# Moving mask products, diagonal chunks and low-part products within TensorE's order in an attention kernel

## What is computed

```python
q = (_rms_norm(x @ w_qa, q_a_norm_w) @ w_qb)          # 16 heads, 128 plain + 64 rotary features
kv = x @ w_kva                                        # 64 latent + 64 rotary features
...
scores = jnp.einsum('bhsd,bhtd->bhst', q_full, k_full) * scale
mask = jnp.tril(jnp.ones((seq, seq), bool))
scores = jnp.where(mask[None, None], scores, jnp.finfo(scores.dtype).min)
attn = jax.nn.softmax(scores, axis=-1)
out = jnp.einsum('bhst,bhtd->bhsd', attn, v)
return out.transpose(0, 2, 1, 3).reshape(b, seq, H * D_V) @ w_o
```

## Time and profile before

| | before |
|---|---|
| median of 3 executions | 1333.49 us (1332.36 to 1334.62) |
| the profiled execution, its own time | 1329.14 us |
| its span | 1327.3 us |
| mean granted clock of TensorE, as a share of 2.4 GHz | 0.958 |
| TensorE matmul busy, of the span | 1208.6 us, 91% |
| VectorE, ScalarE, GpSimd busy | 889.2, 790.8 and 688.2 us |

### The profile page before, as it was taken

One profiled execution on the slowest core, in us unless ns is written; L12 is line 12 of the kernel. 1 busy time (PEld: TensorE's weight loads), 2 busy tenths in 40 slices (PEclk: granted clock), 3 DMA queues, 4 the chain that ended last, 5 costly groups with the idle time before them and its releaser, 6 DMA issues. The chain is left out here.

```text
span 1327.3 us, 23952 instructions
## 1 busy us (share of the span) xinstructions
PE 1208.6 (91%) x9452; PEld 957.0 (72%) x9452; DVE 889.2 (67%) x1836; ACT 790.8 (60%) x1166; POOL 688.2 (52%) x569
## 2 busy tenths in 40 slices
PE   2765999999999999999999999999999867989897
PEld 2653677777777677777777777777777666878886
DVE  2533776776676777767677776767766567677676
ACT  1163467777777777777777777777787733222222
POOL 0122366667666666766666676666676742111100
PEclk9876799999999999999999999999999987999899
DMA  9202010000100200110020010002000040000000
GB/s 276 75 0 64 9 42 17 1 17 28 31 17 1 58 2 17 31 28 17 2 58 1 17 36 23 17 1 58 2 17 2 1 159 1 1 16 1 17 17 16
DMA packets 57679, 39.65 MB, mean 30 GB/s; under 512 B 7744, under 2 KB 57152, under 8 KB 57408
## 3 DMA queue, kind: packets, MB, share of 16 engines
q1 hardware_dynamic: 51216, 33.94, 8.8%
q10 hardware_dynamic: 6352, 4.19, 1.3%
HBM read 33.66 MB, written 4.46 MB: 29 GB/s over the span
## 5 line engine op out<-in xcount | busy, mean ns | idle before, releaser
L777 DVE TENSOR_REDUCE gates<-bank 128x1 f32<-128x512 f32 (+3 forms) x640 | 384.5, 608 | 218.8 <-PE bank L850 144.9
L669 POOL TENSOR_TENSOR pt_lo<-pt 128x1024 f16<-128x1024 f32 x192 | 371.1, 1938 | 227.8 <-ACT pt L726 227.0
L726 ACT ACTIVATE pt<-pair 128x1024 f32<-128x1024 f32 x192 | 196.3, 1023 | 135.8 <-PE pair L875 134.7
L717 ACT ACTIVATE pair<-shift 128x1024 f32<-128x1024 f32 x256 | 263.4, 1029 | 12.2 <-ACT pt L730 0.4
L893 PE MATMUL bank<-values,pt 128*128 128x129 f16 x2176 | 235.1, 222 | 10.1 <-DVE rowsum L809 10.0
L893 PEld LDWEIGHTS bank<-values,pt 128*128 128x128 bf16 x2176 | 191.5, 97 | 62.2 <-issue 34.4
L895 PE MATMUL bank<-values,pt_lo 128*128 128x65 f16 x2176 | 223.8, 192 | 0.0
L675 POOL TENSOR_TENSOR pt_lo<-pt 128x512 f16<-128x512 f32 (+3 forms) x256 | 178.8, 721 | 72.1 <-ACT pt L730 71.6
L895 PEld LDWEIGHTS bank<-values,pt_lo 128*128 128x128 f16 x2176 | 193.8, 98 | 0.0
L730 ACT ACTIVATE pt<-pair 128x512 f32<-128x512 f32 (+3 forms) x256 | 111.5, 437 | 76.9 <-PE pair L878 76.5
L875 PE MATMUL pair<-q_hi,kt_a_hi 128*128 128x512 f32 (+1 forms) x320 | 134.6, 421 | 0.0
(11 more groups left out here) (217 smaller groups left out, 2331.0 us busy)
## 6 DMA issues: line engine op xcount, KB each, us to landing
turn_by<-rope_cos_by_feature SPq DMA_DIRECT2D x64, 128.0 KB, 3.0
turn_by<-rope_sin_by_feature SPq DMA_DIRECT2D x64, 128.0 KB, 3.1
xs<-in_L_attn_x ACTq DMA_DIRECT2D x1, 2048.0 KB, 24.9
lat<-in_L_attn_w_o SPq DMA_DIRECT2D x1, 2048.0 KB, 26.3
xs_again<-in_L_attn_x SPq DMA_DIRECT2D x1, 2048.0 KB, 8.1
out<-xs_again SPq DMA_DIRECT2D x4, 512.0 KB, 2.8
lat<-in_L_wmod SPq DMA_DIRECT2D x1, 1536.0 KB, 15.7
lat<-in_L_attn_w_qb SPq DMA_DIRECT2D x1, 1152.0 KB, 7.6
```

The costliest lines, as they stand in the source:

```text
L669: pool.tensor_tensor(out=pt_lo[:, at].rearrange("p a n -> p (a n)"), in0=full, in1=cut(full), op=ALU.subtract).then_inc(low_ok, 1)
L717: act.activation(s_pair[u % 2][:, :, :], shift[:, item % SHIFTS:item % SHIFTS + 1, :].to_broadcast([P, 2, BW]), ACT.Copy).then_inc(seeded[ ...
L726: act.activation(pt[:, at], s_pair[u % 2][:, :, :], ACT.Exp).then_inc(exp_done, 1)
L777: dve.tensor_reduce(out=mx[:, item % MAXIMA, t, part:part + 1], in_=work_of(w)[:, 0:n * P], axis=AXX, op=ALU.max).then_inc(work_seen["v"], 1)
```

## The change

Three edits. In `scores`, both mask products of a diagonal unit are issued before the unit's first score product, behind the wait for the seed and ahead of the wait for the low part of the queries; the product with the stop flag is now the third score product. In the plan, the chunks of an item are put in another order: the rounds of the chunk numbers stay as they are, but the four diagonal chunks take those numbers that are last in a round of at least two chunks with no shift rows and no query products (`before_values`: there `weigh` follows directly); where an item has fewer than four such places, its earliest other numbers fill up. In `weigh`, the product with the low part comes before the one with the high part. No operation, wait or byte is added or taken away.

```diff
+def before_values(c):
+    r = CHUNK_ROUND[c]
+    return c == CHUNKS_AT[r][-1] and len(CHUNKS_AT[r]) > 1 and r not in SHIFT_AT and PREP_AT.get(r, (0, 3))[1] == 3
+
+for _k in range(NI):
+    _at = range(FIRST_CHUNK[_k], FIRST_CHUNK[_k + 1])
+    _rest = [CHUNKS[c] for c in _at if CHUNKS[c][2] != ITEMS[_k][1]]
+    _diagonal = [CHUNKS[c] for c in _at if CHUNKS[c][2] == ITEMS[_k][1]]
+    _places = sorted(_at, key=lambda c: not before_values(c))[:BT]
+    for _c in _at:
+        CHUNKS[_c] = (_diagonal if _c in _places else _rest).pop(0)
...
                         pe.wait_ge(seeded[e], SEEDS[e][u + 1])
+                        for n in range(0 if d is None else 2):
+                            on = (d + n) * P
+                            pe.matmul(s_pair[u % 2][:, n, on:on + P], mask16[:, :], ident16[:, :], start=False, stop=False,
+                                      skip_group_check=True)
                         if u == FIRST_UNIT[item]:
                             pe.wait_ge(q_lo_ok, item + 1)
...
-                        last = pe.matmul(to, keys[a], q[b], start=False, stop=(m == 2 and d is None), skip_group_check=True)
-                    if d is not None:
-                        on = (d + half) * P
-                        last = pe.matmul(s_pair[u % 2][:, half, on:on + P], mask16[:, :], ident16[:, :], start=False, stop=True,
-                                         skip_group_check=True)
+                        last = pe.matmul(to, keys[a], q[b], start=False, stop=(m == 2), skip_group_check=True)
                     last.then_inc(s_done, 1)
...
-                            pe.matmul(to[:, col:col + 2 * KVL + 1], cut(pt[:, at, half, mine]), values[:, j + half, 0:2 * KVL + 1],
+                            pe.matmul(to[:, col + KVL:col + 2 * KVL + 1], pt_lo[:, at, half, mine], values[:, j + half, KVL:2 * KVL + 1],
                                       start=(u == FIRST_UNIT[item] and half == 0 and t % 2 == 0), stop=False, skip_group_check=True)
-                            last = pe.matmul(to[:, col + KVL:col + 2 * KVL + 1], pt_lo[:, at, half, mine],
-                                             values[:, j + half, KVL:2 * KVL + 1], start=False, stop=end, skip_group_check=True)
+                            last = pe.matmul(to[:, col:col + 2 * KVL + 1], cut(pt[:, at, half, mine]),
+                                             values[:, j + half, 0:2 * KVL + 1], start=False, stop=end, skip_group_check=True)
```

## The result

| | before | after |
|---|---|---|
| median | 1333.86 us (4 runs, 1332.36 to 1334.62) | 1312.74 us (4 runs, 1310.41 to 1314.08) |
| ratio, 95% interval | | 0.9843 (0.9828 to 0.9859) |
| the profiled execution and its span | 1329.14 and 1327.3 us | 1310.41 and 1308.6 us |
| first to last value product (the attention stage) | 155.99 to 1067.66: 911.7 us | 157.46 to 1050.21: 892.8 us |
| all the rest of the span | 415.7 us | 415.9 us |

The change is faster by 21.1 us of the medians, 18.7 us of the two spans. The forecast was 15.3 us and 1318 us; the range 1305 to 1327 holds the result. All of the spans' difference lies in the attention stage. That stage is the finer measure here: a second profile of the changed kernel gave 892.7 us for it (another 0.1 us apart), while the rest took 420.6 us instead of 415.9.

What follows compares the result with a forecast made beforehand. TensorE's queue was taken to bound attention; masks 13.4, low part first 2.9 and chunk order -1.0 summed to 15.3 us, so 1333.49 - 15.3 = 1318 us. The range for 8 in 10 was 1305 to 1327.

Steps and rivals of the forecast that it cites:

- The bound: Attention: TensorE busy 891.7 of 910 us at full clock, so attention costs what its queue costs.
- Masks in front: Diagonal units: two masks behind the value products share one return to fp32r; 20.5 us at most, 13.4 us kept.
- The split by the wait for VectorE: Diagonal rounds: 61 gain 0.16 us each; of 67 with late work, 52 keep 0.04 and 15 keep 0.10.
- Low part first: 192 units off the diagonal: 129-column value product last before fp32r, step 0.04, 2.9 us gained, between 0 and 5.8.
- the estimate by the Trainium skill: Low part first: fp32r load hides behind the whole longer product, 27 ns x 192 = 5.2 us gained instead of 2.9.
- Diagonal chunks last: Chunk order: TensorE gains 1 us, VectorE loses 2; together 1 us lost, between 4 gained and 5 lost.
- VectorE's loss: Rounds with shifts and queries: maxima of full chunks move in, 0.3 x 7 such rounds, 2 us lost.
- (a): Attention rounds: waits don't grow as VectorE is earlier too; 22 to 30 us gained, 1303.5 to 1311; chance 0.19.
- (b): Masks in front: transition moved, not saved, or VectorE holds the next unit; 2.7 to 9 us left, 1324.5 to 1331; chance 0.12.
- (c): Work banks were the bound all along, savings become waits; 1333 us give or take 2.7; chance 0.06.
- (d): Round of group 0's second unit: VectorE becomes the bound, 4 us slower, 1337 to 1338; chance 0.05.

Runs made afterwards that it cites:

- e1: Only the two masks moved in front of the unit's first score product, against the kernel before; attention stage 11.0 us shorter.
- e9: Changed kernel with shift rows and query products behind the round's weighing, except the third query product, kept ahead of it; 1293.62 us, ratio 0.9698, stage 872.0 us.
- e4: Masks in front and low part first, chunk order as before, against the kernel before; 1312.3 us.

## Why the prediction was right, and where its sizes were off

**The bound** was read right. TensorE's queue limits attention, and a product's price is its distance to the next start. The edits changed the returns to fp32r, 734 in the trace before and 433 after, as counted from the loops, and the time followed.

**Masks in front**: 13.4 us forecast, 11.0 measured by e1's stage. Both kinds of rounds behaved as said, 0.136 on average where 0.16 was forecast (50 of 60 rounds near it, 10 far below) and 0.047 where 0.04 and 0.10 were. The split by the wait for VectorE, without which the forecast would have been 20.5, is the step that the size hangs on; e9 shows the wait itself. The two masks cost 0.06 and 0.03, as said within 0.01.

**Low part first**: 2.9 us forecast, 4.1 measured (e4 against e1). The term was mis-sized: the step of a 129-column product before fp32r was taken as 0.04, from the mask's row as the nearest one, and it is 0.03 (561.55 to 561.58 above). With 0.028 x 192 TensorE's part is 5.4, near the upper bound of 5.8, and the stage shows 4.1 of it. The forecast's argument against the estimate by the Trainium skill was that the first fp32r product takes 0.32 behind a mask as behind a 65-column product. That stayed so, and it does not speak against the estimate: what got shorter is the step of the 129-column product itself, 0.06 to 0.03, and not the product behind it (0.31 to 0.32 in all). The estimate of 5.2 was nearer to TensorE's part; from the measured stage it is as far as 2.9 is (1.1 and 1.2 us).

**Diagonal chunks last**: 1 us lost forecast, 3.9 us gained measured (2.1 alone). This is the step that failed, by its sign. TensorE's part was put at 1 us, VectorE's loss at 2 us in the round of group 0's second unit. That round did not grow: 2.20 before, 2.16 after. In its place the order took away two waits for the reading out of the output banks, 3.1 us (e4 against the changed kernel), each behind a spread of 2.4 us on VectorE that had begun just behind a GpSimd operation. The forecast took VectorE's operations at fixed durations, and had no term in which one of them takes 0.69 or 2.4 us by what GpSimd does. What is left of the gain, some 0.8 us, is near the 1 us put down for TensorE, but it is a balance of larger shifts between rounds.

**The sum**: 15.3 forecast; 13.4, 2.9 and -1.0 became 11.0, 4.1 and 3.9, together 19.0 in the stage. The errors partly cancel: 2.4 too much for the masks, 6.1 too little for the other two. And 3.1 of the 19.0 hang on which of two operations starts first by less than 0.1 us, in two rounds; that part of the gain is luck, in the change as in the forecast. The forecast's mechanism for the masks and for low first is borne out. The rivals: (a), in which no wait takes its part, wanted 0.16 in every diagonal round, and those with late work gained 0.047; (b) wanted a second transition in front, which isn't there (one 0.32, behind the second mask), and a time of 1324.5 or more; (c) and (d) are out by the result.

## What to carry to other kernels

Where TensorE's queue is full, price a product by the start distance in each place it can stand: a 128-column bf16 product costs 0.13 us between fp32r products here and 0.06 among 16-bit ones, and as the last of several 16-bit products before an fp32r one it costs 0.03, the same with 65 and with 129 columns. Before counting on a gain, look for a fixed latency that spans the place (a bank that comes back 1.27 us after a chunk): what is saved inside it is not saved. Filling that latency with work that was behind it brought as much as the reordering itself, from 1314 to 1294 us, and the two together 1288 us, 3.4% below the kernel before. And compare round by round before giving a gain to a rule: two rounds of 317 held most of what the chunk order brought.

## What was not expected of the hardware

A VectorE operation of 0.69 us (the spread) takes 2.4 when a GpSimd operation has begun 0.04 to 0.09 us before it, and GpSimd's 1.90 becomes 2.44 when the spread is first. 64 more columns in the last product before an fp32r one cost nothing (0.9992, 0.9983 to 1.0002). An fp32r mask product is a little cheaper than a bf16 one in fp32r company, 0.11 against 0.13 us. And with the attention stage equal to 0.1 us, two profiles of the same kernel differ by 4.8 us in the rest, with a granted clock of 1.00 in one and 0.91 in the other between 1140 and 1180 us.
